# The last head pair of an attention kernel takes the common path through VectorE and DMA, and GpSimd takes the FFN's small work

## What is computed

```python
xn      = layernorm(x)                                # x (2, 256, 256)
q       = einsum(xn @ Wq.T, w_kc_q, W_qr)              # 16 heads of 64
kv_rope = rope(ctx_512)                                # (2, 512, 64), one for all heads
k       = einsum('bld,hdr->bhlr', kv_rope, W_kr)
attn    = softmax(einsum('bhsr,bhlr->bhsl', q, k))     # (2, 16, 256, 512)
ctx     = einsum('bhsl,bld->bshd', attn, kv_rope)
x       = x + einsum('bhsd,hkd->bshk', ctx, w_kc_kv).reshape(2, 256, 2048) @ Wo.T
soft    = sigmoid(pweight) - sigmoid(nweight)          # (256, 256, 4)
weight  = einsum('oin,n->oi', soft, exps * sigmoid(mask_weight)) * scale
bias    = round_to_4_bits(einsum('on,n->o', pbias - nbias, bexps)) * biasscale
x       = x + layernorm(x) @ weight.T + bias
```

## Time and profile before

| | |
|---|---|
| device time, median of 3 | 136.69 us (136.23 to 137.05) |
| device time of the profiled execution | 136.4 us |
| its span | 134.6 us |
| TensorE's mean granted clock | 0.998 |
| PE busy | 127.3 us, 95% |
| DVE busy | 105.7 us, 79% |
| POOL busy | 85.5 us, 64% |
| ACT busy | 75.5 us, 56% |

### The profile page before, as it was taken

How to read it: one execution, slowest core, us unless ns; L and a number is a source line. 1 busy time by engine, 2 the same in 40 slices (tenths; PEclk the granted TensorE clock), 3 DMA queues, 4 the chain that set the end, 5 groups by cost and what they waited for, 6 DMA issues and landing times.

```text
span 134.6 us, 2532 instructions
## 1 busy us (share of the span) xinstructions
PE 127.3 (95%) x910; PEld 90.5 (67%) x910; DVE 105.7 (79%) x159; ACT 75.5 (56%) x192; POOL 85.5 (64%) x126
## 2 busy tenths in 40 slices
PE   6989799999889999999999999999999999999992
PEld 6767589467657767666576676666675686766770
DVE  0387844999999684996999699699969799997092
ACT  4242643769459382937638475983976673544110
POOL 6507957969989939296957959677585643004240
PEclk9999999999999999999999999999999999999999
DMA  3899987999999799899989999999889980000004
GB/s 81 232 336 216 154 135 256 231 125 211 233 252 249 150 217 211 207 297 276 245 234 305 261 249 282 239 262 309 227 234 178 267 221 23 5 0 0 0 0 156
DMA packets 29132, 26.13 MB, mean 194 GB/s; under 512 B 17056, under 2 KB 20768, under 8 KB 29120
## 3 DMA queue, kind: packets, MB, share of 16 engines
q1 hardware_dynamic: 26992, 22.84, 69.3%
q0 software_dynamic: 1456, 2.77, 9.0%
q10 hardware_dynamic: 672, 0.36, 0.9%
HBM read 10.50 MB, written 0.52 MB: 82 GB/s over the span
## 4 chain that ended last, share of the span: by engine, by line
PE 75%; DVE 9%; ACT 8%; DMA 4%; SPq 1%; issue 1%; ACTq 0%; DVEq 0%
PE score L968 18%; PE ctxb L984 16%; PE ctxb L939 8%; PE proj L994 8%; ACT probs L451 6%; DVE neg_max L650 4%; PE score L1128 4%; DMA ctx_rows<-in_ctx_dram 4%; PE foldb L904 3%; PE foldb L919 3%; DVE turned L666 2%; PE score L1153 1%; PE score L1106 1%; PE foldb L1128 1%; PE ctxb L950 1%; DVE bulk L615 1%
## 5 line engine op out<-in xcount | busy, mean ns | idle before, releaser
L451 ACT ACTIVATE probs<-score,neg_max 128x512 f32<-128x512 f32 x64 | 43.2, 686 | 28.8 <-DVE neg_max L650 28.8
L389 POOL TENSOR_SCALAR probs<-probs,row_inv 128x512 f32<-128x512 f32 x64 | 43.9, 735 | 23.8 <-DVE row_inv L656 23.8
L650 DVE TENSOR_REDUCE neg_max<-score 128x2 f32<-128x1024 f32 x32 | 37.6, 1216 | 10.9 <-PE score L968 10.9
L968 PE MATMUL score<-k_t,q_t 64*128 64x256 f32 x256 | 32.7, 391 | 1.5 <-ACT probs L451 1.4
L666 DVE STREAM_TRANSPOSE turned<-probs 128x1024 f32<-128x1024 f32 x28 | 33.0, 1216 | 0.0
L968 PEld LDWEIGHTS score<-k_t,q_t 64*128 64x128 f32 x256 | 23.2, 186 | 8.9 <-ACT probs L451 3.7
L381 POOL DMA_DIRECT2D wo<-in_L_xattn_Wo_dram x32 | 28.0, 1019 | 0.0
L984 PE MATMUL ctxb<-spread,kv 128*64 128x256 f32 x192 | 22.0, 382 | 0.0
L984 PEld LDWEIGHTS ctxb<-spread,kv 128*64 128x64 f32 x192 | 13.3, 137 | 8.0 <-issue 2.0
L939 PE MATMUL ctxb<-hq_t,m 128*128 128x512 f32 x28 | 13.7, 611 | 0.0
L451 ACT ACTIVATION_READ_ACCUMULATOR probs<-score,neg_max 128x1 f32 x64 | 13.0, 203 | 0.0
(11 more groups left out here) (144 smaller groups left out, 149.3 us busy)
## 6 DMA issues: line engine op xcount, KB each, us to landing
spread<-turned SPq DMA_DIRECT2D x56, 256.0 KB, 5.5
wo<-in_L_xattn_Wo_dram POOLq DMA_DIRECT2D x32, 64.0 KB, 5.0
wq<-in_L_xattn_Wq_dram SPq DMA_DIRECT2D x1, 1280.0 KB, 13.7
bulk<-in_L_ffn_pweight_dram SPq DMA_DIRECT2D x2, 512.0 KB, 6.2
bulk<-in_L_ffn_nweight_dram SPq DMA_DIRECT2D x2, 512.0 KB, 7.2
bulk<-in_L_xattn_w_kc_q_dram SPq DMA_DIRECT2D x4, 192.0 KB, 8.7
wq<-in_L_xattn_Wq_dram SPq DMA_DIRECT2D x1, 512.0 KB, 7.4
wkv<-in_L_xattn_w_kc_kv_dram SPq DMA_DIRECT2D x1, 512.0 KB, 5.9
```

What stands on the lines that cost most here:

```text
L389: pool.tensor_scalar(p, p, row_inv[:, j:j + 1], 1.0, ALU.mult, ALU.mult).then_inc(norm_made, 1)
L451: act.activation(probs[:, j, :], score[u % 2][:, h, :], ACT.Exp, bias=neg_max[:, j:j + 1], accum_out=row_sum[:, j:j + 1]).then_inc(exp_mad ...
L650: dve.tensor_reduce(neg_max[:, j:j + 2], score[u % 2][:], axis=AX, op=ALU.max, negate=True)\
L968: product = pe.matmul(score[u % 2][:, h, half * S:half * S + S], q_t[rows, i % 2, b, tt * P:tt * P + P], k_t[rows, b, half * S:half * S + ...
```

## The change

1. **The last pair** goes through `turn_two` on DVE and `spread_probs` on SP like the others (`for i in range(NP)`). `transpose_probs`, `take_transposed`, `kv_turned` and its four transfers are gone.
2. **GpSimd** makes the scales (`weight_scales`, behind `normalise(10)`), the first difference (`ffn_difference(0)`, behind `normalise(11)` and two `load_wo`), the bias (`bias_values`, behind `normalise(12)`) and the second difference (behind `normalise(13)`).
3. **DVE** sums the first two bits of the first 128 rows at the head of pair 6 (`first_bits(0)`) and the rest at the head of pair 7 (`last_bits(0)`); the second 128 rows follow behind the last turns and `early_residual`.
4. **`wo`** is loaded one pair earlier from pair 3 on (pair 2 loads two), and nothing is loaded in pair 6. The first tanh moves from pair 5 to pair 4.
5. **The key transposes** read a stored permutation `key_ident` in place of a strided view of `ident`.
6. **The end** on PE: `values_side(7)`, the bias products, `projections(5)`, late contexts of pair 6, their projection, late contexts of pair 7 batch 0, the transposed FFN weights, its projection, late contexts of pair 7 batch 1, and then as before.

```diff
@@ sync
-            for i in range(LASTP):
+            for i in range(NP):
                 for half in range(2):
                     spread_probs(i, half)
-                if i == 0:
...
-                    for k in range(G):
-                        sp.dma_start(kv_turned[k * BK:k * BK + BK, :, :], kv[k:P:G, :, 0:DC]).then_inc(kv_moved, 16)
@@ gpsimd
+            pool.wait_ge(ident_made, 1)
+            pool.tensor_copy(key_ident[:].rearrange("p (k c) -> p k c", k=G),
+                             ident[:].rearrange("p (c k) -> p k c", k=G)).then_inc(key_ident_made, 1)
...
+            def weight_scales():
...
+                link(pool.tensor_scalar(bits[:, 3, :], mask_t[:], 0.5, 0.5, ALU.mult, ALU.add))
+                link(pool.tensor_tensor(bits[:, 3, :], bits[:, 3, :], bits[:, 0, :], ALU.mult))
+                pool.tensor_scalar(bits[:, 3, :], bits[:, 3, :], scales[:, 0:1], 0.5, ALU.mult, ALU.mult)\
+                    .then_inc(scales_made, 1)
...
+            def ffn_difference(ot):
+                pool.wait_ge(tanh_made, 2 * ot + 2)
+                pool.tensor_tensor(pw[:, ot, :], pw[:, ot, :], nw[:, ot, :], ALU.subtract).then_inc(difference_made, 1)
...
-                        elif i < LASTP and j // 2 == half:
-                            load_wo(i + 1, j)
+                        elif i < SECOND and j // 2 == half:
+                            load_wo(i + 1 if i < 3 else i + 2, j)
+                            if i == 2:
+                                load_wo(4, j)
+                    if i == 5 and half == 0:
+                        weight_scales()
+                    elif i == 5:
+                        ffn_difference(0)
+                    elif i == SECOND and half == 0:
+                        bias_values()
+                    elif i == SECOND:
+                        ffn_difference(1)
@@ scalar
-                if i in (5, 6):
+                if i in (4, 6):
@@ vector
+            def first_bits(ot):
+
+                dve.wait_ge(difference_made, ot + 1)
+                dve.wait_ge(scales_made, 1)
...
             for i in range(1, LASTP):
                 u, v = SLOTS * i, 2 * i
+                if i == SECOND:
+                    first_bits(0)
                 maxima(u)
...
             u, v = SLOTS * LASTP, 2 * LASTP
+            last_bits(0)
             maxima(u)
...
-            ffn_difference(0)
+            turn_two(v, 0)
             inverses(v + 1)
-            ffn_scales()
-            ffn_weights(0)
-            ffn_difference(1)
-            ffn_weights(1)
+            turn_two(v, 1)
+            turn_probs(v + 1)
...
             early_residual(T - 1)
+            first_bits(1)
+            last_bits(1)
@@ tensor
                     last = pe.transpose(key_bank[b][:, lt * P:lt * P + P], kv[:, b * LT + lt, :],
-                                        ident[:].rearrange("p (c k) -> p k c", k=G))
+                                        key_ident[:])
```

More of the change, by code:

```diff
@@ L128, in xattn_ffn_kernel @@
         ident = sb("ident", [P, P])
+        key_ident = sb("key_ident", [P, P])
         warm = sb("warm", [P, 1])
@@ L159, in xattn_ffn_kernel @@
         spread = [sb(f"spread{k}", [P, G, TILES, LT, BK]) for k in range(2)]
-        kv_turned = ctx_rows
-        probs_t = turned[LASTP % 2][:].rearrange("p g j l r -> p (g j l r)")\
-            .rearrange("p (b l h s) -> p b l h s", b=B, l=LT, h=2)
         ctx_t = sb("ctx_t", [P, T * P])
@@ L185, in xattn_ffn_kernel @@
         early, late = score[0], score[1]
[L186 to L188 removed]
+        late_ctx_bank = [[late[:, 0, :], late[:, 1, :]], [early[:, 0, :], fold_bank[:]]]
         bias_bank = early[:, 1, :]
@@ L243, in xattn_ffn_kernel @@
         tanh_made = sem("tanh_made")
+        scales_made = sem("scales_made")
+        difference_made = sem("difference_made")
         ffn_w_made = sem("ffn_w_made")
@@ L580, in _ @@
                .then_inc(ffn_w_taken, 1)
-            take_hidden(0)
-            take_hidden(1)
             take_late_contexts(LASTP, 1, 4)
-            take_hidden(2)
-            take_hidden(3)
+            for t in range(T):
+                take_hidden(t)
         @block.vector
@@ L656, in inverses, with turn_two @@
                 dve.reciprocal(row_inv[:, j:j + 4], row_sum[:, j:j + 4]).then_inc(inv_made, 1)
+            def turn_two(v, n):
+                i, half, j = v // 2, v % 2, 4 * (v % 2) + 2 * n
+                if i >= 2 and n == 0:
+                    dve.wait_ge(probs_spread[i % 2][half], landed(i - 2))
+                dve.wait_ge(norm_made, 4 * v + 2 * n + 2)
+                dve.transpose(turned[i % 2][:, :, j:j + 2, :, :].rearrange("p k j l r -> p (j l) k r"),
+                              probs[:, j:j + 2, :].rearrange("p j n -> p (j n)")).then_inc(probs_turned, 1)
@@ L684, in ffn_difference @@
[L684 to L688 removed]
+                    turn_two(v, n)
+            def first_bits(ot):
+                dve.wait_ge(difference_made, ot + 1)
+                dve.wait_ge(scales_made, 1)
                 w_bits = pw[:, ot, :].rearrange("o (i n) -> o i n", n=NB)
                 link(dve.tensor_scalar(w_ffn[:, ot, :], w_bits[:, :, 0], bits[:, 3, 0:1], None, ALU.mult))
[L692 to L695 removed]
+                link(dve.scalar_tensor_tensor(w_ffn[:, ot, :], w_bits[:, :, 1], bits[:, 3, 1:2],
+                                              w_ffn[:, ot, :], ALU.mult, ALU.add))
@@ L696, in ffn_weights, with last_bits @@
+            def last_bits(ot):
+                w_bits = pw[:, ot, :].rearrange("o (i n) -> o i n", n=NB)
+                for n in range(2, NB):
+                    link(dve.scalar_tensor_tensor(w_ffn[:, ot, :], w_bits[:, :, n], bits[:, 3, n:n + 1],
+                                                  w_ffn[:, ot, :], ALU.mult, ALU.add))
                 link(dve.bn_stats(w_stats[:, ot, :], w_ffn[:, ot, :]))
@@ L1122, in late_contexts @@
                 for lt in range(LT):
                     for h in range(2):
-                        if i == SECOND:
-                            rows, columns = kv[:, b * LT + lt, h * DC:h * DC + DC], spread_columns(i, b, h, lt)
-                        else:
-                            rows, columns = kv_turned[:, b * LT + lt, :], probs_t[:, b, lt, h, :]
-                        last = pe.matmul(late_ctx_bank[i - SECOND][b][64 * h:64 * h + 64, 0:S], rows, columns,
+                        last = pe.matmul(late_ctx_bank[i - SECOND][b][64 * h:64 * h + 64, 0:S],
+                                         kv[:, b * LT + lt, h * DC:h * DC + DC], spread_columns(i, b, h, lt),
```

149 lines of the change are left out of this document (41 added, 108 removed).

## The result

The changed kernel takes **143.2 us** (median of 4 runs, 142.88 to 145.24), against 136.53 us for the kernel before in the same session (4 runs, 136.23 to 137.05). The ratio is 1.0485, with a 95% interval of 1.0456 to 1.0514: slower by 4.9%. One of its four executions, of 145.24 us, was in a slower state that the kernel before shows at times too, and the ratio leaves it out. The forecast was 142.8 us. The profiled execution took 142.91 us, its span is 141.1 us, and the mean granted clock 0.976 (before 0.998).

What follows compares the result with a forecast made beforehand. PE bounds the kernel; other engines' time is free until PE waits. Last late contexts at 130.0 plus 11.0, less 0.8, plus 0.5: span 140.7; plus 1.8 and 0.3 gives 142.8 us, range 140 to 146.5.

Steps and rivals of the forecast that it cites:

- The border: Pairs 5 and 6: DVE waits for GpSimd's difference, maxima of slot 24 come 6.7 us late, PE stands 5.15 us.
- The small operations at nothing: GpSimd's scales behind `normalise(10)` and bias between `normalise(12)` and `normalise(13)` fit its idle time; taken as 0.
- To pair 7: DVE's work from the maxima of slot 24 to those of slot 28: 12.8 us, ending at 106.5, 7.6 late.
- The contexts of pair 5: On PE, they start 7.6 us late, at 111.8 against 104.24.
- The end: Pair 7's last late contexts wait for DMA and start at 130.0; 11.0 us follow.
- PE alone: PE's own work from the contexts of pair 5 to the last late contexts: 15.2 us, down from 19.5.
- The tail: From the start of the last late contexts to the span's end: 11.0 us, before 10.9.
- The front: Key transposes with a stored permutation are faster, 0.45 us for each of two groups; 0.8 of 0.9 taken, floor 0.
- The clock: TensorE's clock falls to 1.2 GHz in the border wait of 5.15 us; cost 0.5 us, between 0 and 2.5.
- The rival in which the clock costs 2.7 more: Slow clock for 3 us at the end and 1 more lost in pair 6: 145.5 us, chance 0.14.
- The rival without the wait: DVE does not wait at the border of pairs 5 and 6: 135.9 us, faster than before, chance 0.04.
- The edits at nothing: The tanh in pair 4 and the doubled `wo` loads of pair 2 cost nothing.

Runs made afterwards that it cites:

- the two experiments that moved the work: Changed kernel with the first two sums moved to the head of pair 7: 139.55 us; with GpSimd's scales and first difference a half earlier: 139.77 us.
- the kernel with 21 products: Changed kernel plus 21 idle products of 128 columns on TensorE in its wait at the border of pairs 5 and 6: 142.56 us, ratio 1.0411.

## Why the prediction was right, point by point

**The border** was right in mechanism and in size. Predicted: the difference ends at 92.5, maxima of slot 24 at 93.7, PE idle 5.15 from 91.35. Measured: 92.57, 93.78, 5.15. Two terms were off and all but cancelled, which is luck: the difference took 2.73 us and not 2.3, and started at 89.84 and not 90.16, since GpSimd goes on while its issues are still shown. The size is thus near the upper end, four times the row of 256 columns (2.9), not near the straight line (2.1); the second difference took 2.35, and why the two differ is open. The Trainium skill (GPSIMD Engine Reference, section 3.1) had led to an estimate of 2.25, which the second comes near and the first does not.

**The small operations at nothing**: right. The scales take 0.59, 0.20 and 0.28 us and end at 85.54, before `normalise(11)`; the bias runs from 101.24 to 103.68, GpSimd then waits 1.03 for VectorE.

**To pair 7** the term was too small: predicted 12.8 us from 93.7 to 106.5, measured 13.6, to 107.36. The 0.8 are VectorE's pause of 0.28 us for scores at the slow clock, and `last_bits(0)` with 2.83 us for 2.4, as some of its instructions run beside GpSimd's tiles. The prediction's own split was off too: 6.7, plus 2.4 less 1.11, is 8.0 and not the 7.6 that its sum gave. It forgot DVE's other pause, of 0.28 us. That VectorE and GpSimd lengthen each other stood in no term of the sum. In this kernel it cost 0.4 us; in the two experiments that moved the work it cost 2 to 3.

**The contexts of pair 5**: predicted 111.8, measured 112.56, for the same reason.

**The end** came out at the predicted time by two errors. Half 14 was turned at 117.97 (predicted 117.0), half 15 at 120.9 (119.8), both by the lateness above. The transfers were faster: from the first issue to the landing of the last it was 12.0 us (117.99 to 130.03), between the bounds of 11.4 and 14.0, while 13.0 had been taken. 130.08 against 130.0. The new path was worth 2.0 us (19.5 to 17.5) and not 1.3 (to 18.2). PE alone needs 15.9 us of this stretch, by the kernel without the last transfers, where the prediction had 15.2; the transfers hid that error. The tail was 11.0, as predicted.

**The front**: -0.8 was predicted and 0 came, the floor of the range. The step that failed is "since transfers may hold back a part": in this execution they held back all; the kernel with nothing but this edit gained 0.6.

**The clock**: the fall was right; that the trace "shows no slow start" was true of before only. Here PE ran at 0.50 for 5.4 us after its wait. That is the slow start that the Trainium skill (TensorE: Matmul & The Clock Gate, Part 1) states. "Some 2 us after work stops" did not repeat: PE had stood since 91.44, and the clock read 1.00 up to 95.0. The 0.5 us that were taken for it stand against 0.35 in the trace of the kernel with 21 products. The rival in which the clock costs 2.7 more had the waits at the end right (0.81 and 0.71 us), but the clock did not fall there: it reads 1.00 in the last window,

```profile
138.50:141.10 2.60, 0.00 (x0) 0.00 (x0) 0.43 (x1) 0.00 (x0) 0.00 (x0) 1.00 0.57 186
```

where the earlier trace rows had 0.91, though PE had stopped 2.7 us before the end in both.

**The sum**: 130.08 + 11.0 = 141.1 for the span, predicted 140.7; the difference is the front (0.8) less what the clock was given (0.5), and rounding. The rival without the wait adds up to 136.0, not 135.9; the version with the sums at the end, which has no such wait, took 134.5 and 134.3.

**The edits at nothing** that held: the tanh in pair 4 (its two instructions at 73.60, PE busy 11.60 of 11.60 us), and the doubled `wo` loads of pair 2 (PE busy 12.00 of 12.00 us from 46 to 58).

## What to carry to other kernels

An instruction that waits for another engine is paid by all that is queued behind it. Ask first what that other engine must do before, and whether it waits in turn for the instruction just ahead on the first; here one pass through GpSimd behind VectorE's own reciprocal made a loop of 7 us. The same work in a pause of the waiting engine costs next to nothing: the four sums moved behind the last turns turned 4.9% slower into 1.9% faster, with all the rest of the change kept. And before work, or a transfer, is moved to an engine or its queue "because it is idle there", read what stands behind it on that engine.

## What the hardware showed that was not expected

- A VectorE sum of 0.45 us took 2.84, 2.99 and 2.75 us when it started behind the start of a row of four GpSimd tiles, and a subtraction of 0.35 us took 2.25 beside one long GpSimd instruction. With one or two inputs, strided or not, it was the same. The same subtraction, begun in the middle of a row of tiles, took 0.62. Maxima and 32 x 32 turns take the same time beside GpSimd's tiles (2.36 us for two).
- After a wait of PE of 5.15 us the clock stayed at half for about 5.4 us of work, and for about 4.4 after the 4.97 us of the kernel with the sums at pair 7. After waits of 2 us it was not the same each time: kept after 2.01 us, lower for a while after 2.16 and 1.92 (in the second of these the contexts of that half took 4.44 us for 3.67, in the first 4.25). These three put the maxima of slot 28 at 18.0, 18.2 and 17.9 us behind the border, so it changed at most 0.3 us there. In one execution the clock fell after waits of only 1.12 and 0.49 us, and cost 1.6.
- Four DMA issues of 256 KB on ScalarE's queue held the engine for 4.68 us.
- With the key transposes of the changed kernel, the score block that waits for the first weights starts between 38.36 and 39.83 in the traces. That is more than many edits are worth, so stretches between two points in one trace are the better measure.
